# Value products of the third attention made in layer 0's tail and loaded per batch

## The reference

```python
q = jnp.einsum('btd,dnh->btnh', query, Wq) + bq
k = jnp.einsum('bsd,dnh->bsnh', value, Wk) + bk
v = jnp.einsum('bsd,dnh->bsnh', value, Wv) + bv
probs = jax.nn.softmax(scores + adder, axis=-1)
ctx = jnp.einsum('bnts,bsnh->btnh', probs, v)
out = jnp.einsum('btnh,nhd->btd', ctx, Wo) + bo
```

## Time and profile before

| | us |
|---|---|
| median of 3 runs | 1601.33 |
| lowest, highest | 1598.24, 1602.20 |
| profiled execution, span from first to last instruction | 1600.8 |
| TensorE busy in the span | 1386.6 (87%) |
| VectorE busy | 953.2 (60%) |
| ScalarE busy | 664.8 (42%) |

### The profile page before, as it was taken

The page is one execution under the profiler, slowest core; times in us unless marked ns, Lnnn a source line. Parts: engine busy times, 40 slices in busy tenths (PEclk is TensorE's granted clock), DMA queues, the critical chain, the costliest instruction groups (busy, mean ns, idle before and its releaser), DMA issues. The chain is left out here.

```text
span 1600.8 us, 31601 instructions
## 1 busy us (share of the span) xinstructions
PE 1386.6 (87%) x10662; PEld 1150.0 (72%) x10662; DVE 953.2 (60%) x2331; ACT 664.8 (42%) x1313; POOL 422.6 (26%) x578
## 2 busy tenths in 40 slices
PE   8999878889999994999999998999999997401588
PEld 5888645677799983788888887779999996400245
DVE  4888665666422225777777774832222265688887
ACT  3666453420344430333333334335555522430277
POOL 1000000012122210122221221246666633421141
PEclk9999999899799997999999998889999999755799
DMA  3000020673111107111111202012333344421001
GB/s 107 21 20 15 6 92 1 218 268 61 60 34 41 34 22 226 62 51 49 49 47 32 44 1 93 1 52 92 92 93 93 86 173 134 108 19 10 1 14 40
DMA packets 105328, 106.53 MB, mean 67 GB/s; under 512 B 36080, under 2 KB 92160, under 8 KB 105088
## 3 DMA queue, kind: packets, MB, share of 16 engines
q1 hardware_dynamic: 89312, 70.91, 14.6%
q0 software_dynamic: 11136, 28.93, 6.6%
q10 hardware_dynamic: 4768, 5.25, 1.1%
HBM read 83.19 MB, written 20.71 MB: 65 GB/s over the span
## 5 line engine op out<-in xcount | busy, mean ns | idle before, releaser
L3598 PEld LDWEIGHTS L2f_bank<-L2f_xT,L2f_w_tile 128*128 128x128 f32 x1264 | 154.5, 193 | 7.4 <-ACT L2f_xT L3662 3.4
L3598 PE MATMUL L2f_bank<-L2f_xT,L2f_w_tile 128*128 128x128 f32 x1264 | 155.2, 276 | 3.0 <-ACT L2f_xT L3662 3.0
L785 POOL TENSOR_TENSOR L2x_probs<-L2x_probs,L2x_inv_sum 128x512 f32<-128x512 f32 x64 | 66.3, 1057 | 268.4 <-DVE L2x_inv_sum L1062 268.4
L3712 DVE TENSOR_TENSOR L2f_hT<-L2f_gate_h,L2f_bank 128x256 f32<-128x256 f32 x79 | 33.3, 421 | 148.5 <-ACT L2f_gate_h L3669 148.5
L3521 POOL DMA_INDIRECT L2f_y_rows<-L2f_xn,L2f_put_row x79 | 78.2, 989 | 55.2 <-DVE L2f_xn L3728 51.6
L3656 ACT COPY L2f_w_tile<-L2f_w_up 128x1024 f32 x79 | 82.7, 1046 | 17.4 <-issue 17.4
L3513 POOL DMA_INDIRECT L2f_rows<-L2f_x_rows,L2f_take_row x79 | 77.0, 975 | 44.7 <-DVE L2f_take_row L3496 21.3
L3598 PEld LDWEIGHTS L1f_bank<-L1f_xT,L1f_w_tile 128*128 128x128 f32 x736 | 85.6, 192 | 1.1
L3598 PE MATMUL L1f_bank<-L1f_xT,L1f_w_tile 128*128 128x128 f32 x736 | 85.9, 275 | 0.0
L3615 PE MATMUL L1f_bank<-L1f_w_down,L1f_hT 128*128 x368 | 83.1, 379 | 0.0
L3615 PE MATMUL L2f_bank<-L2f_w_down,L2f_hT 128*128 x316 | 81.4, 380 | 0.1
(11 more groups left out here) (677 smaller groups left out, 3321.2 us busy)
## 6 DMA issues: line engine op xcount, KB each, us to landing
L1f_w_up<-in_L_ffn_w SPq DMA_DIRECT2D x16, 512.0 KB, 8.2
L1f_w_down<-in_L_ffn_w SPq DMA_DIRECT2D x16, 512.0 KB, 9.0
L2f_got<-L2f_y_rows SPq DMA_DIRECT2D x16, 512.0 KB, 4.4
L2f_w_up<-in_L_ffn_gate_w SPq DMA_DIRECT2D x16, 256.0 KB, 2.9
L2f_w_up<-in_L_ffn_up_w SPq DMA_DIRECT2D x16, 256.0 KB, 3.0
L2f_w_down<-in_L_ffn_down_w SPq DMA_DIRECT2D x16, 256.0 KB, 3.6
x<-in_x SPq DMA_DIRECT2D x4, 512.0 KB, 7.9
L0x_ctx<-in_ctx SPq DMA_DIRECT2D x16, 128.0 KB, 2.1
```

The lines of the kernel that those rows point to most:

```text
L785: nc.gpsimd.tensor_tensor(probs[c][:, :, :], probs[c][:, :, :], inv_sum[:, c, :][:, :, None].to_broadcast([P, 4, P]), ALU.mult).then_inc(s ...
L3598: x = nc.tensor.matmul(products(j, m), w_tile[j][:, at:at + P], xT[j][:, k * P:(k + 1) * P], start=(k == 0), stop=(k == KT - 1))
L3712: nc.vector.tensor_tensor(hT[j][:, 0:F], gate_h[j][:, 0:F], bank[2 + j][:, F:2 * F], ALU.mult).then_inc(q["h"], 1)
```

## The change

The value products leave the third attention. In the first attention SyncE also loads `Wv` (two transfers of 512 KB) and, for each batch, copies the transposed context out of `xcT` to a buffer that lives through layer 0 (16 KB in each partition). ScalarE, before it overwrites `xcT`, waits for the copy of two batches before.

In the depth block's tail, the 32 value units (a unit is two matmuls of 512 columns: 16 batches x two halves) are made behind the down products: 20 of them before the wait for VectorE's results, 12 one by one behind the first 12 returns. The units use banks 4 to 7 and the returns banks 0 to 3, so a return waits for the addition of four batches before and not of eight. ScalarE copies each unit into one of four row buffers, and SyncE stores each batch's 512 KB to memory. The four filler matmuls at the end are gone.

In the third attention each batch's values are loaded from memory, behind context and mask and ahead of the expert weights in SyncE's queue, once the weighting of batch b-2 is made. There are five fills (T, Q0, K0, Q1, K1) and not seven, and `wv` is not loaded.

```diff
+class ValuesAhead:
+    HALVES = 2
+    BUFS = 4
+    W = 1024
...
+    def make(self, u, dst, ks=range(KT)):
+        b, half = u // self.HALVES, u % self.HALVES
+        for k in ks:
+            t = self.core.nc.tensor.matmul(dst[:, :], self.ctxT[:, b, k * P:(k + 1) * P], self.half(self.w[:, k, :], half),
+                                           start=(k == 0), stop=(k == KT - 1))
+        return t
...
 # first attention, SyncE
+            def keep(j, b):
+                sp.wait_ge(s["evicted"], b * NF + (T + 1))
+                settle(sp, s["passed"])
+                sp.dma_start(values.ctxT[:, bass.ds(b, 1), :].rearrange("p a c -> p (a c)"),
+                             xcT[j][:, KT:, :].rearrange("p t c -> p (t c)")).then_inc(s[f"kept{j}"], 16)
...
                 load_inputs(j, b)
+                keep(j, b - 2)
...
 # first attention, ScalarE
                 if f == T:
+                    if not (isinstance(b, int) and b < 2):
+                        act.wait_ge(s[f"kept{j}"], loads(b - 2, j))
...
 # third attention
-    fills = ["T", "Q0", "K0", "Q1", "K1", "V0", "V1"]
+    fills = ["T", "Q0", "K0", "Q1", "K1"]
...
                 load_inputs(j, b)
+                sp.wait_ge(s["pv"], (b - 1) * 2)
+                settle(sp, s["passed"])
+                load_values(j, b)
                 ahead.part(sp, b)
...
             def weighted(j, b, r):
                 if r == 0:
-                    evicted(pe, b, fills.index("V0"))
-                else:
-                    evicted(pe, b, fills.index("V1"))
+                    pe.wait_ge(s[f"v_in{j}"], loads(b, j))
...
 # depth block
+        def take_value(act, u):
+            b, half = u // 2, u % 2
+            act.wait_ge(v["made"], u + 1)
+            after(act, v[f"stored{b % values.BUFS}"], 16 * (b // values.BUFS))
+            nc.scalar.copy(values.half(values.rows[b % values.BUFS], half), bank[value_bank[u]][:, :]
+                           ).then_inc(v["taken"], 1)
+
+        def store_values(sp, b):
+            sp.wait_ge(v["taken"], 2 * b + 2)
+            sp.dma_start(values.dram[b], values.rows[b % values.BUFS][:, :]).then_inc(v[f"stored{b % values.BUFS}"], 16)
...
-            return bank[b % 8][:, 0:D]
+            return bank[b % 4][:, 0:D]
...
+            def tail_value(u):
+                after(pe, v["taken"], u - 3)
+                make_value(u)
+
+            first = UNITS - (B - 4)
+            for u in range(first):
+                tail_value(u)
+
             pe.wait_ge(t1["result"], G)
             for b in range(B):
                 g, odd = b % 8 // 2, b % 2
-                after(pe, t1["updated"], b - 7)
+                after(pe, t1["updated"], b - 3)
                 nc.tensor.matmul(back_of(b), pickT[odd][32 * g:32 * g + 32, b // 8 * P:(b // 8 + 1) * P],
                                  result[32 * g:32 * g + 32, b // 8, :], start=True, stop=True).then_inc(t1["back"], 1)
-
-            pe.wait_ge(t1["updated"], B - 7)
-            stay_warm(core, bank[(B - 8) % 8], 4)
+                if b < B - 4:
+                    tail_value(first + b)
```

More of the change, by code:

```diff
@@ L284, in take_stats, with __init__, half, narrow_attention @@
     return core.nc.vector.bn_stats(cols(core.stats, b * 6, 6), cols(core.x, b * D, D))
-def narrow_attention(core):
+class ValuesAhead:
+    HALVES = 2
+    BUFS = 4
+    W = 1024
+    def __init__(self, core, v_dram, ctx):
+        self.core, self.dram = core, v_dram
+        sb = core.sbuf_in(ctx)
+        self.ctxT = sb("ahead_ctxT", [P, B, KT * P])
+        self.w = sb("ahead_wv", [P, KT, self.W])
+        self.rows = [sb(f"ahead_rows{j}", [P, self.W]) for j in range(self.BUFS)]
+    def half(self, rows, half):
+        at = self.W // self.HALVES
+        return rows[:, half * at:(half + 1) * at]
+    def make(self, u, dst, ks=range(KT)):
[4 more added lines that the diff above has]
+        return t
+def narrow_attention(core, values):
     nc, ins = core.nc, core.ins
@@ L354, in _ @@
                     body(j, i * 2 + j)
+            for b in range(B - 2, B):
+                keep(b % 2, b)
+            sp.wait_ge(s["values_w"], 16 * KT)
+            for j in range(2):
+                sp.wait_ge(s[f"kept{j}"], 16 * B // 2)
         @block.gpsimd
@@ L826, in front @@
                 half = int(kind[1])
-                if kind[0] == "V":
+                w, of = (wq, 0) if kind[0] == "Q" else (wk, KT)
+                for i in range(4):
+                    t = 4 * half + i
                     for k in range(KT):
-                        last = nc.tensor.matmul(dst[:, :], xcT[j][:, KT + k, :], wv[:, k, half * 512:(half + 1) * 512],
-                                                start=(k == 0), stop=(k == KT - 1))
-                else:
[L832 to L837, removed]
+                        last = nc.tensor.matmul(dst[:, i * P:(i + 1) * P], w[:, k, t * P:(t + 1) * P],
+                                                xcT[j][:, of + k, :], start=(k == 0), stop=(k == KT - 1))
                 last.then_inc(s["filled"], 1)
@@ L903, in body @@
                 if not last:
-                    for f in range(3, NF - 1):
+                    for f in range(3, NF):
                         front(1 - j, b + 1, f)
@@ L942, in take @@
                 src = front_bank[(j * NF + f) % 2]
-                kind = fills[f]
                 act.wait_ge(s["filled"], b * NF + f + 1)
[L946 to L953, removed]
+                nc.scalar.copy(xcT[j][:, :, :].rearrange("p t c -> p (t c)"), src[:, :]).then_inc(s["evicted_act"], 1)
             def exp(b, r, c):
@@ L1182, in depth_routed_block, with make_value @@
             "placed", "pick", "aug", "U", "U_out", "pickT", "mask_in"])
+        v = core.sems_in("L0v", ["made", "taken"] + [f"stored{j}" for j in range(values.BUFS)])
         phases = Phases(nc)
+        UNITS = 2 * B
+        value_bank = [4 + u % 4 for u in range(UNITS)]
+        def make_value(u, ks=range(KT)):
+            t = values.make(u, bank[value_bank[u]], ks)
+            if KT - 1 in ks:
+                t.then_inc(v["made"], 1)
+        def take_value(act, u):
[7 more added lines that the diff above has]
+            sp.dma_start(values.dram[b], values.rows[b % values.BUFS][:, :]).then_inc(v[f"stored{b % values.BUFS}"], 16)
         block = phases.open()
@@ L1595, in _ @@
             nc.scalar.preload_act_table(ACT.Sqrt)
+            for u in range(UNITS):
+                take_value(act, u)
         @block.vector
```

49 lines of the change are left out of this document (27 added, 22 removed).

## The result

The changed kernel took 1613.74 us (median of 4 runs, 1610.28 to 1618.36), the kernel before beside it 1599.87 (4 runs, 1598.24 to 1602.2): a ratio of 1.0094, 95% interval 1.007 to 1.0119. It is slower by some 14 us, as forecast (1611, range 1599 to 1618).

The account below looks back on a forecast made before the run. TensorE, 87% busy, was taken to set the pace in the third attention. 1600.8 + 52.4 (layer 0's tail) + 1.6 (clock) - 43.7 (third attention) = 1611.1 us, said as 1611; range 1599 to 1618.

Parts of the forecast that it names:

- the wait that was named: Third attention: TensorE waits 1.0 us a batch before line 818's transposes for VectorE's normalisation.
- The unit: Layer 0's tail: two matmuls of 512 columns cost 1.73 us, priced from the down products; upper bound 1.82 to 1.92.
- The rounds: Layer 0's tail: twelve rounds of one return and one unit, 2.26 us each, with 0.1 for the change of shape.
- The end of the tail: Layer 0: the last 512 KB store lands after 4.4 us, at 341.2, and closes the stage after VectorE's 339.7.
- The clock: Start of the next stage: four of six fillers at half rate after TensorE's pause, 1.6 us later; bounds 0 and 2.6.
- The period: Third attention: a loop through VectorE and TensorE sets 18.15 us a batch instead of 21.17, gaining 3.02.
- Start and end of the stage: Third attention, outside the 13 periods: 2.4 us gained at the start and 2.0 at the end.
- Layer 0's attention, ScalarE, loads and stores: Added weights, batch copies, ScalarE's wait and value loads cost nothing; copies, if exposed, 2 us a batch, loads 4.4.
- rival D: Layer 0's attention: copies and weights are exposed after all, 14 x 0.5 us, 1618 us; chance 0.04.
- E: Third attention: values not taken early enough, a wait of 0.5 us a batch at the weighting, 1618 us; chance 0.04.
- C: Layer 0's tail: stores bound it at one per 5 us, 80 us instead of 62, 1629 us; chance 0.05.
- Rival B: Third attention: TensorE stays the bound, the stage gains 56.4 us, time 1598.4 us; chance 0.19.

Follow-up runs that it names:

- e6: Changed kernel with the tail's returns made four batches together, then four value units, three times, instead of one and one twelve times; 1610.11 us, ratio 1.006.
- e1: Changed kernel with the third attention of the kernel before; the tail still makes and stores values that nobody reads; 1662.25 us, ratio 1.0399.
- e3: Changed kernel with the projection of batch b-1 put ahead of the waiting transposition on TensorE in the third attention; 1620.59 us, ratio 1.0119.
- e3b: e3 with ScalarE making each half's exponentials before it copies the transposed weights; 1605.44 us, ratio 1.0046.
- e5: Changed kernel with VectorE normalising the rows of batch b+2 before the first-half sums of b+1 in the third attention; 1619.48 us, ratio 1.0129.
- e8: Changed kernel with the grouped tail of e6 and the third attention of e3b, without filler matmuls at the tail's end; 1601.34 us, ratio 0.9995.
- e9: The changed kernel unaltered, run and profiled again; 1616.05 us, ratio 1.0096 to the kernel before.

## Why the prediction was right, and where its terms were off

The sum was +52.4 +1.6 -43.7 = +10.3; the two profiles show +11.9. The mechanism was right: the value products cost their full price in the tail, and the third attention gave three of the four microseconds a batch, held by the wait that was named. That the sums agree within 1.6 us is in part luck.

- **The unit**: 1.73 predicted, 1.72 measured. The price came from the down products beside it in the trace, scaled by columns, and not from the 1.82 to 1.92 of the third attention, which hold a change of shape.
- **The rounds, the mis-sized term**: 2.26 predicted, 2.54 measured, 12 x 0.28 = 3.4 us. The step that was off is "with 0.1 for the change of shape": against the same prices of unit and return it is 0.38. e6, with nine changes fewer, got 6.1 us, of which some 3.4 go to the changes and the rest to returns that overlap (estimates, see e6).
- **The end of the tail**: the last store was to end it, at 4.4 us. It lands in 2.6 and VectorE ends it, 3.96 us after the last round (3.7 predicted). By the loads' row the store was 1.8 too dear; the lower bound, had VectorE last. The same page has other loads of 512 KB, which the prediction did not weigh: 8.2 and 9.0 us for layer 1's weights and 7.9 for x. By the dearest the term would have been 4.6 us larger, so the choice of row was fortunate. Together the tail's last work is at 343.5 and not 341.2. The estimate of 3.2 us that I had from the Trainium skill (DMA: Bandwidth & Descriptors, Anatomy of one DMA, given there for GpSimd's path) was nearer than the row, and 0.6 too high for this store on SyncE's queue; the measurement decides.
- **The barrier, which the sum had left at its old price**: from the last needed instruction to the next stage 2.27 us before, because the old fillers ran on past VectorE's end, and 1.12 after. That is 1.15 us gained.
- **The clock**: 1.6 predicted, 2.65 measured (5.46 against 2.81), after TensorE had stood still for 3.94 us and not for about 6. All six fillers ran at half rate in this execution and in e6, the upper bound of that term. In the six others without fillers at the end of the tail (e1, e3, e3b, e5, e8, e9) it is 1.5 to 1.7, the term as predicted.
- **The period**: 18.15 predicted, 18.22 measured (718.99 to 955.88 in 13 batches), with the wait that was named, in front of the instruction that was named, 0.84 us instead of 1.0. Thirteen periods give 38.4 instead of 39.3. "More than 1 us of room" in VectorE's chain was too much: its one pause there is 0.61, at the key copy, and in e3 its loop was the bound at 18.17.
- **Start and end of the stage**: a gain of 1.5 and 2.6 us instead of 2.4 and 2.0. At the start TensorE idles 4.76 us for VectorE's sums of the bias products, not 2.49, and runs at half rate until the query products (3.19 us for 16 records, 1.95 later).
- **Layer 0's attention, ScalarE, loads and stores**: the transposes of the third and of the last batch of the first attention start 130.7 us apart before and 130.6 after, and 130.6 to 130.8 in all twelve profiles, so copies and loads cost a batch nothing, and rival D's 0.5 us did not come about. Nobody waits for a load of values (E), nor ScalarE for a store (C, whose price of 1629 lay outside the stated range).
- **What is left open**: the third attention and the tail explain 13.4 us. In ten of the eleven comparisons the medians differ by more than these two stages do, by 0.5 to 8 us. The kernel before has one profile only, so a small cost elsewhere can't be told from the spread of executions.
- **Rival B** asked for TensorE alone as the bound, at 17.17 a batch. It takes two edits of order, one on TensorE and one on ScalarE, to come there (e3b), and then the period is 17.49.

So the profile's 1.6 us over the sum are: rounds +3.36, the twenty units -0.14, the end with VectorE in place of the store -1.24, the barrier -1.15, layer 0 ahead of the tail +0.31, the clock +1.00, the attention +1.26, and -1.83 in layer 1 and the rest, which the forecast had at nothing. Terms of both signs cancelled, and the last one is no larger than what two executions differ by.

Why there is nothing to gain: the 64 matmuls cost TensorE their full time at either place. In e8, with nine of the changes of shape and the loop's waits removed, the tail is 48.9 us longer than before and the third attention 51.9 shorter, and the medians are equal. What the changed kernel loses is what e8 takes away, 14.7 us on one chip: the waits of the loop (10.7 us of the stage in e3b) and the single rounds (6.1 in e6).

## What to carry to other kernels

Work taken off the bounding engine is worth its full length only until the next loop closes. Shift the schedule by hand until every wait is met, including those that would come out at zero: here two bounds lay some 0.1 us apart, and the list of waits named one. Work moved into another stage of the same engine has to be paid there, so ask first how much of that stage is truly idle, and put alternating matmuls of two shapes in groups. Before a difference of two rows is called the cost of something, look whether both rows run alone or beside others. When you move an instruction that waits, look at what every other engine has queued behind the work that now comes later.

## What the runs showed of the hardware that I had not expected

- A change between matmuls of 32x256 and 128x512 and back cost 0.38 us a round (2.54 against 1.73 + 0.43), nearly four times my value.
- Returns with an operand of 32 rows overlap when they follow each other: their records start in pairs 0.01 us apart, and four returns take 1.07 us, where a lone one takes 0.63 (changed kernel and e6).
- A store of 512 KB from SyncE's queue lands in 2.6 us and a load in 3.4, against 4.4 for the row of a load of the same size in another stage.
- Two executions of one program differ by 4.9 us before 275 us and by 3.9 in layer 1, with the granted clock (0.91 and 0.78 in one stretch of 20 us) as the difference that the rows show. Over all twelve profiles the first mark lies between 264.0 and 274.4 us. Medians of 6 to 12 runs still carry an interval of 0.2 to 0.35% to either side.
